# A gated attention and routed-expert kernel on one core: weight chunks split during the first stage, base products before the gather, quantisation maxima in PSUM

## The chip, the cores and the metric

The program runs on one core of one Trainium2 chip. The core has five engines with a queue each: TensorE (PE, matrix products and transposes into PSUM), VectorE (DVE), ScalarE (ACT), GpSimd (POOL) and SyncE (SP, which here only issues DMAs). Work in different queues is ordered by semaphores alone; inside one queue it runs in the order in which it was written. The metric is device time in microseconds (us) of one launch; less is better.

## The reference, cut to what matters

Two residual blocks follow each other on 4 x 256 tokens of width 256. The first is an int8 "smooth quant" two-layer product (four batches), the second routes every token to 2 of 8 experts.

```python
def _smooth_quant_linear(x, w):
    amax_x, amax_w = jnp.max(jnp.abs(x), axis=0), jnp.max(jnp.abs(w), axis=0)
    s = jnp.maximum(jnp.sqrt(jnp.maximum(amax_x, EPS) / jnp.maximum(amax_w, EPS)), EPS)
    xs, ws = x / s, w * s
    x_scale = jnp.maximum(jnp.max(jnp.abs(xs), axis=-1, keepdims=True), EPS) / QMAX
    w_scale = ...                      # the same over ws
    return round(xs / x_scale) @ round(ws / w_scale).T * x_scale * w_scale.T

x = x + tanh(g_xattn) * smooth_quant_expert(layernorm(x), fside, ctx)      # first stage
x2 = layernorm(x)
conf = sigmoid(x2 @ conf_W.T + conf_b); sel, routing = top-2 of conf * wealth
base_g, base_u = x2 @ base_gate, x2 @ base_up                              # 256 -> 896, all tokens
for e in range(8):
    g = base_g + x2 @ gate_A[e] @ gate_B[e] / 4
    u = base_u + x2 @ up_A[e] @ up_B[e] / 4
    h = silu(g) * u
    out += weight_e * (h @ base_down + h @ down_A[e] @ down_B[e] / 4)
x = x + tanh(g_ffn) * out
```

## The kernel before

There are two stages and a routing plan between them.

**First stage.** Each of the four batches b runs the same chain: layer norm, transposes on TensorE, maxima over the transposed banks on VectorE (`weights_amax`, `rows_amax`, `gated_amax`, `context_amax`), square roots on GpSimd (`roots1`, `roots2`), scaling on ScalarE, products, dequantisation, residual, a second layer norm (`stats2`, then `deviations2` on GpSimd, then `normal2` on ScalarE). The four batches are interleaved by hand: every engine's queue is written out call by call. Maxima go to small SBUF tiles (`amx`, `am1`, `am2`), from which a chain of small VectorE instructions (`ratio`: maximum with EPS, reciprocal, product, maximum; L894 to L899) makes the factors.

**Weights of the second stage.** They are needed as pairs of rounded numbers (`_hi`, `_lo`). SyncE loads them in 41 chunks of at most 128 x 512 through a ring `raw` of 4 slots. ScalarE copies a chunk to `_hi` (`split`, L579), GpSimd subtracts to get `_lo` (`split_lo`, L440), and only then is the slot loaded again (L391). Chunks 0 to 7 are base_gate and base_up, 8 to 11 the A matrices, 12 to 20 down_A and down_B, 21 to 28 gate_B, 29 to 36 up_B (`CH_1` is 37), the last four base_down. On GpSimd 12 chunks are placed among the calls of the first stage, then `lo(CH_1 - lo_done[0])` (L505) does the other 25. The first two gathers stand behind that line in the same queue.

**Base products.** `base_half(t, gu)` on TensorE makes one half (gate or up) of the 256 -> 896 product of token tile t (8 tiles): 12 products of 448 columns. ScalarE copies each half to `brow` and stores it to HBM. Tiles 0 to 5 (`PRE` is 6) stand ahead of the plan; tiles 6 and 7 stand behind the transposition `x_T(0)` of the first gathered tokens.

**The plan.** Logits of the four batches (`conf_rows`, then the transposes at L1472), sigmoid, top 2 on VectorE (L1038 to L1052, giving `pickb`), ranks on TensorE (L1483 to L1487, `s_rank`), places on VectorE (L1066 to L1080), two one-hot tables (`atrow` L1081, `attrib` L1083 to L1088), a sorting product on TensorE (L1496, `s_sorted`), and the indices `tok` and `dest` (L1106, `s_plan`).

**Second stage.** 19 tiles of 128 token-expert pairs: gather (`gather`, L511), project, expand, silu, product, transpose (`h_T`, L1548), down products, scatter. Tile 0 makes its base products directly from the gathered rows (L1606 to L1610, `s_direct`), because the stored rows are not ready then; `gather_base` fetches them for later tiles and waits for `s_direct`.

## Time and profile before

| | us |
|---|---|
| median of 3 runs | 347.58 (346.81 to 350.02) |
| the profiled execution's own time | 349.11 |
| its span, first to last instruction | 347.2 |
| TensorE busy | 261.5 (75%) |
| VectorE busy | 201.3 (58%) |
| ScalarE busy | 167.1 (48%) |
| GpSimd busy | 133.8 (39%) |

The busy shares are means over stages that have different limits. The page also prints the span in 40 slices of 8.7 us (each digit is the busy share in tenths; PEclk is the clock that TensorE was granted, in tenths of full speed):

```profile
PE   2569547988981003995999999999999999997700
POOL 5396614220057995018233333333333333311111
PEclk9855997899996555898999999999999999999755
```

TensorE has nothing to do in slices 12 to 15, which are the same slices in which GpSimd is full. Behind them the second stage holds TensorE at nine tenths until almost the end.

### The profile page before, as it was taken

How to read it: one execution, taken by the hardware profiler on the slowest of the kernel's cores; microseconds unless marked ns; L12 is line 12 of the kernel's file. 1: busy time of each engine (PE TensorE's matmuls, PEld its weight loads, DVE VectorE, ACT ScalarE, POOL GpSimd, SP SyncE). 2: the span in 40 equal slices, each digit the busy share in tenths (PEclk: the TensorE clock that was granted, in tenths of full speed). 3: DMA queues.
4: the chain of work that ended last, by engine and by line, in shares of the span. 5: the costliest groups of instructions: out<-in, count | busy, mean ns of one | idle time of the engine just before them, and what ended most of it. 6: DMA issues, size and time to landing. Idle time of an engine off the chain costs nothing.

```text
span 347.2 us, 5197 instructions
## 1 busy us (share of the span) xinstructions
PE 261.5 (75%) x1540; PEld 236.1 (68%) x1541; DVE 201.3 (58%) x409; ACT 167.1 (48%) x285; POOL 133.8 (39%) x162
## 2 busy tenths in 40 slices
PE   2569547988981003995999999999999999997700
PEld 1446435877971002994999999999999999996600
DVE  4598997661497000016667767777777677776115
ACT  2448875756354351253555545555555555555011
POOL 5396614220057995018233333333333333311111
PEclk9855997899996555898999999999999999999755
DMA  8545210025348674226244444444444444400065
GB/s 255 166 124 124 62 31 30 32 106 206 161 154 248 189 206 127 105 120 217 83 135 146 139 130 137 142 138 139 143 141 135 144 137 138 145 21 15 17 205 173
DMA packets 30190, 45.69 MB, mean 132 GB/s; under 512 B 13976, under 2 KB 25632, under 8 KB 30176
## 3 DMA queue, kind: packets, MB, share of 16 engines
q0 software_dynamic: 4416, 21.50, 18.7%
q1 hardware_dynamic: 21840, 14.55, 14.8%
q10 hardware_dynamic: 3920, 9.46, 7.2%
q8 instruction: 8, 0.13, 0.2%
q14 instruction: 6, 0.05, 0.0%
HBM read 33.57 MB, written 11.93 MB: 131 GB/s over the span
## 4 chain that ended last, share of the span: by engine, by line
PE 62%; DVE 10%; DMA 10%; POOL 6%; ACT 6%; issue 3%; SPq 2%; ACTq 0%; DVEq 0%
PE pY L55 8%; PE pY L59 7%; PE pY L57 7%; PE pG L55 5%; PE pT L1548 4%; PE pG L57 4%; PE pG L59 4%; PE pU L57 3%; PE pU L59 3%; PE pU L55 3%; DMA q<-in_ctx_dram 3%; PE bank L1254 2%; DMA yr<-results 2%; DMA raw<-in_L_ffn_down_A_dram 2%; POOL WdA_lo L440 2%
## 5 line engine op out<-in xcount | busy, mean ns | idle before, releaser
L525 POOL DMA_INDIRECT results<-yb,dest x19 | 18.8, 987 | 94.4 <-DVE yb L1188 94.4
L55 PE MATMUL pY<-Wd_hi,hT_hi 128*128 128x384 f32 x133 | 48.3, 363 | 1.1 <-ACT Wd_lo L789 0.8
L59 PE MATMUL pY<-Wd_hi,hT_lo 128*128 128x384 f32 x133 | 45.3, 341 | 0.0
L57 PE MATMUL pY<-Wd_lo,hT_hi 128*128 128x384 f32 x133 | 45.3, 341 | 0.0
L519 POOL DMA_INDIRECT bin<-base_products,tok x18 | 22.0, 1220 | 26.9 <-PE pU L59 17.1
L799 ACT CAST hT_hi<-pT 128x896 fp32r<-128x896 f32 x19 | 17.2, 907 | 24.1 <-PE pT L1548 24.1
L1511 PE MATMUL pX<-ident,xin 128*128 128x128 f32 x38 | 7.5, 280 | 27.9 <-DMA xin<-normed,tok 27.9
L55 PEld LDWEIGHTS pY<-Wd_hi,hT_hi 128*128 128x128 f32 x133 | 25.4, 191 | 3.3 <-issue 1.0
L775 ACT CAST xaT_hi<-pX 128x256 fp32r<-128x256 f32 x19 | 7.1, 374 | 42.5 <-PE pX L1525 42.1
L1118 DVE TENSOR_TENSOR xT_lo<-pX,xT_hi 128x256 fp32r<-128x256 f32 x19 | 7.9, 416 | 31.0 <-ACT xT_hi L769 31.0
L57 PEld LDWEIGHTS pY<-Wd_lo,hT_hi 128*128 128x128 f32 x133 | 25.6, 193 | 0.0
L59 PEld LDWEIGHTS pY<-Wd_hi,hT_lo 128*128 128x128 f32 x133 | 25.5, 191 | 0.0
L1511 PEld LDWEIGHTS pX<-ident,xin 128*128 128x128 f32 x38 | 5.3, 143 | 29.5 <-issue 28.0
L1261 PE MATMUL bank<-ident,q 128*128 128x128 f32 x80 | 16.9, 361 | 11.1 <-DMA q<-in_fside_BxS2xS_dram 6.4
L1172 DVE TENSOR_TENSOR hbuf<-hbuf,gb 128x896 f32<-128x896 f32 x19 | 22.6, 1192 | 1.9
L511 POOL DMA_INDIRECT xin<-normed,tok x19 | 18.6, 981 | 11.6 <-PE pX L1511 6.7
L1176 DVE TENSOR_TENSOR hT_lo<-pT,hT_hi 128x896 fp32r<-128x896 f32 x19 | 20.5, 1082 | 2.8 <-ACT hT_hi L799 2.8
L1261 PEld LDWEIGHTS bank<-ident,q 128*128 128x128 f32 x80 | 12.5, 185 | 14.2 <-issue 4.3
L1548 PE MATMUL pT<-ident,hbuf 128*128 128x128 f32 x133 | 18.4, 280 | 4.2 <-DVE hbuf L1172 4.2
L1145 DVE TENSOR_TENSOR xaT_lo<-pX,xaT_hi 128x256 fp32r<-128x256 f32 x19 | 8.1, 424 | 23.1 <-ACT xaT_hi L775 23.1
L793 ACT ACTIVATE gb<-gb 128x896 f32<-128x896 f32 x19 | 18.1, 954 | 6.6 <-DVE gb L1159 6.4
L1182 DVE TENSOR_TENSOR zT_lo<-pX,zT_hi 128x128 fp32r<-128x128 f32 x19 | 5.5, 292 | 25.9 <-ACT zT_hi L806 25.9
(234 smaller groups left out, 778.4 us busy)
## 6 DMA issues: line engine op xcount, KB each, us to landing
base_products<-brow ACTq DMA_DIRECT2D x8, 896.0 KB, 3.6
yr<-results SPq DMA_DIRECT2D x8, 256.0 KB, 5.4
raw<-in_L_ffn_down_A_dram SPq DMA_DIRECT2D x7, 256.0 KB, 3.0
raw<-in_L_ffn_gate_B_dram SPq DMA_DIRECT2D x8, 224.0 KB, 2.8
...
```

Of the source, the lines that this page charges most:

```text
L55: m.matmul(outs[i], hi, whi[i], start=first, stop=False, skip_group_check=True)
L57: m.matmul(outs[i], hi, wlo[i], start=False, stop=False, skip_group_check=True)
L59: ins = m.matmul(outs[i], lo, whi[i], start=False, stop=last, skip_group_check=True)
L511: g.indirect_dma_start(out=xin[:, :], out_offset=None, in_=xn, in_offset=bass.IndirectOffsetOnAxis(ap=tok[:, j:j + 1], axis=0)).then_inc(d ...
L519: g.indirect_dma_start(out=bin_[:, j % 2].rearrange("p a i -> p (a i)"), out_offset=None, in_=gun, in_offset=bass.IndirectOffsetOnAxis(ap= ...
L525: g.indirect_dma_start(out=yg, out_offset=bass.IndirectOffsetOnAxis(ap=dest[:, j:j + 1], axis=0), in_=yb[:, :], in_offset=None).then_inc(d ...
L793: a.activation(gb[:, :], gb[:, :], ACT.Silu).then_inc(s_silu, 1)
L799: a.copy(hT_hi[:, :, :].rearrange("p c q -> p (c q)"), pT[:, :, :].rearrange("p a q -> p (a q)")[:, 0:I]).then_inc(s_hhi, 1)
L1172: v.tensor_tensor(hbuf[:, :], hbuf[:, :], gb[:, :], ALU.mult).then_inc(s_h, 1)
L1176: v.tensor_tensor(hT_lo[:, :, :].rearrange("p c q -> p (c q)"), pT[:, :, :].rearrange("p a q -> p (a q)")[:, 0:I], hT_hi[:, :, :].rearrang ...
L1261: ins = m.transpose(bank[:, c * S + j * P:c * S + (j + 1) * P], rows_[:, j, c * P:(c + 1) * P], ident[:, :])
L1548: ins = m.transpose(pT[:, c // 4, (c % 4) * P:(c % 4 + 1) * P], hbuf[:, c * P:(c + 1) * P], ident[:, :])
```

## The change

It does four things. Splits are placed among the calls of the first stage and of the plan on ScalarE and GpSimd, and the ring has 6 slots. Base products of tiles 6 and 7 stand ahead of the plan's last wait, the rank products come one half earlier, and tile 0's direct products are split in two around `xa_T(0)`. Maxima are left in PSUM and the quotient chains have fewer instructions (reciprocals of the weights' and context's maxima are made ahead in `rcp_w` and `rcp_c`; the epsilon of the layer norm is added by a reduction). Nothing is left out of the computation.

```diff
-        RING, RW = 4, 512
+        RING, RW = 6, 512
@@ gpsimd, behind roots1(3) and lo(1)
             roots2(1)
+            lo(4)
             gated(2)
             deviations2(0)
+            lo(1)
             roots2(2)
+            lo(1)
             gated(3)
             deviations2(1)
+            lo(1)
             roots2(3)
+            lo(4)
             deviations2(2)
+            lo(1)
             deviations2(3)
             lo(CH_1 - lo_done[0])
@@ scalar
             integers_w(2)
-            split(1)
+            split(3)
             scaled2(0)
             scales_w(2)
             integers2(0)
+            split(1)
             scales_c(0)
+            split(1)
...
             normal2(0)
+            split(1)
             scales_w(3)
             x2_hi(0)
+            split(1)
             silu1(3)
+            split(2)
...
             integers2(2)
+            split(1)
...
             integers2(3)
+            split(1)
             base_half(1, 0)
             scales_c(3)
+            split(1)
             normal2(2)
             base_half(1, 1)
             base_store(1)
+            split(1)
             x2_hi(2)
             normal2(3)
...
             conf_rows(3)
+            split(1)
             act.wait_ge(s_logit, 1)
             a.activation(bids[:, :, :], bids[:, :, :], ACT.Sigmoid).then_inc(s_sig, 1)
+            split(2)
             base_half(3, 0)
+            split(1)
             base_half(3, 1)
             base_store(3)
+            split(2)
             base_half(4, 0)
...
             base_half(5, 1)
             base_store(5)
-            split(2)
             split(CH_1)
+            for t in range(PRE, NT):
+                base_out(t)
...
             x_hi(0)
-            for t in range(PRE, NT):
-                base_out(t)
             xa_hi(0, first=True)
@@ vector
             def weights_amax(b):
                 dve.wait_ge(s_wT, b + 1)
-                v.tensor_reduce(amx[:, b, 1, :], ...).then_inc(s_wamax, 1)
+                v.tensor_reduce(amx_w[:, b, :, 0], ...).then_inc(s_wamax, 1)
+                dve.wait_ge(s_wamax, b + 1)
+                link(v.tensor_reduce(rcp_w[:, b, :], amx_w[:, b, :, :], AX_X, ALU.max))
+                link(v.reciprocal(rcp_w[:, b, :], rcp_w[:, b, :]))
             def context_amax(b):
                 dve.wait_ge(s_cT, b + 1)
-                v.tensor_reduce(amx2[:, b, 1:2], beta(b)[:, 0:S], ...).then_inc(s_camax, 1)
+                c = beta(b)[:, S + 8:S + 9]
+                link(v.tensor_reduce(c, beta(b)[:, 0:S], AX_X, ALU.max, apply_absolute_value=True))
+                link(v.tensor_scalar(c, c, EPS, None, ALU.max))
+                v.reciprocal(rcp_c[:, b:b + 1], c).then_inc(s_camax, 1)
@@ statistics
-                v.tensor_scalar(vs, vs, LN_EPS, None, ALU.add).then_inc(made, 1)
+                v.tensor_reduce(wide[:, TB * b:TB * (b + 1)], mine[:, :, 1:3], AX_X, ALU.add).then_inc(made, 1)
@@ rows_amax; gated_amax likewise
-                ratio(amx[:, b, 0, :], amx[:, b, 1, :], amx[:, b], tmp8[:, b, :], s_ratio)
+                link(v.scalar_tensor_tensor(out=x_, in0=x_, scalar=EPS, in1=rcp_w[:, b, :], op0=ALU.max, op1=ALU.mult))
+                v.tensor_scalar(tmp8[:, b, :], x_, EPS * EPS, None, ALU.max).then_inc(s_ratio, 1)
@@ smooth1; smooth2 likewise
-                link(v.tensor_reduce(am1[:, b, :], q1[:, :, b, :], AX_X, ALU.max, apply_absolute_value=True))
-                scales(am1[:, b, :], inv1[:, b, :], sc1[:, b, :], s_inv1)
+                am = beta(b)[:, 0:4]
+                link(v.tensor_reduce(am, q1[:, :, b, :], AX_X, ALU.max, apply_absolute_value=True))
+                scales(am, inv1[:, b, :], sc1[:, b, :], s_inv1)
@@ tensor
             base_half(3, 1)
-            base_half(4, 0)
             pe.wait_ge(s_pickb, 1)
...
             ins.then_inc(s_rank, 1)
-            base_half(4, 1)
-            base_half(5, 0)
-            base_half(5, 1)
+            base(4)
+            base(5)
+            base_half(6, 0)
...
             ins.then_inc(s_sorted, 1)
+            base_half(6, 1)
+            base(7)
             pe.wait_ge(s_plan, 1)
...
             x_T(0)
-            base(PRE)
             pe.wait_ge(s_wlo, CH_A)
             project_A(0, group(0))
-            base(PRE + 1)
+            direct(0)
             xa_T(0)
-            for gu, copied in enumerate((s_bgc, s_buc)):
-                ...
-            ins.then_inc(s_direct, 1)
+            direct(1).then_inc(s_direct, 1)
```

What the change does to the queues stands at three places. The first is GpSimd's queue from the last square root of the first stage to the first gather (`_lo` rows are weight chunks, `rstd` and `nmr` the layer norm). Before:

```order
L476 TENSOR_TENSOR s_rs<-tmp,half 128x2
L453 TENSOR_TENSOR rstd<-mv,half 128x2
L456 TENSOR_SCALAR nmr<-mv,rstd 128x1 x2
L453 TENSOR_TENSOR rstd<-mv,half 128x2
L456 TENSOR_SCALAR nmr<-mv,rstd 128x1 x2
L440 TENSOR_TENSOR WdA_lo<-raw,WdA_hi 128x512 x7
L440 TENSOR_TENSOR WdB_lo<-raw,WdB_hi 128x512 x2
L440 TENSOR_TENSOR WBg_lo<-raw,WBg_hi 128x448 x8
L440 TENSOR_TENSOR WBu_lo<-raw,WBu_hi 128x448 x8
L511 DMA xin<-normed,tok 128x256 x2
```

With the change:

```order
L481 TENSOR_TENSOR s_rs<-tmp,half 128x2
L445 TENSOR_TENSOR WdB_lo<-raw,WdB_hi 128x512 x2
L445 TENSOR_TENSOR WBg_lo<-raw,WBg_hi 128x448 x2
L458 TENSOR_TENSOR rstd<-spread,half 128x2
L461 TENSOR_SCALAR nmr<-mv,rstd 128x1 x2
L445 TENSOR_TENSOR WBg_lo<-raw,WBg_hi 128x448
L458 TENSOR_TENSOR rstd<-spread,half 128x2
L461 TENSOR_SCALAR nmr<-mv,rstd 128x1 x2
L445 TENSOR_TENSOR WBg_lo<-raw,WBg_hi 128x448 x5
L445 TENSOR_TENSOR WBu_lo<-raw,WBu_hi 128x448 x8
L522 DMA xin<-normed,tok 128x256 x2
```

Of the 25 chunks that stood in one piece ahead of the gather 12 are now among the first stage's calls and 13 are left; five of the 12 stand ahead of the last two layer norms.

The second place is TensorE's queue at the rank products (`bank<-pickb` is their first row; `pG` and `pU` rows are base halves). Before:

```order
L59 MATMUL pU<-Wbase_hi,x2T_lo 128x448 x2
L55 MATMUL pG<-Wbase_hi,x2T_hi 128x448 x2
L57 MATMUL pG<-Wbase_lo,x2T_hi 128x448 x2
L59 MATMUL pG<-Wbase_hi,x2T_lo 128x448 x2
L55 MATMUL pG<-Wbase_hi,x2T_hi 128x448 x2
L57 MATMUL pG<-Wbase_lo,x2T_hi 128x448 x2
L59 MATMUL pG<-Wbase_hi,x2T_lo 128x448 x2
L1483 MATMUL bank<-pickb,beforeb 128x64
```

With the change:

```order
L57 MATMUL pU<-Wbase_lo,x2T_hi 128x448 x2
L59 MATMUL pU<-Wbase_hi,x2T_lo 128x448 x2
L1511 MATMUL bank<-pickb,beforeb 128x64
L1513 MATMUL bank<-pickb,onesb 128x60
L1513 MATMUL bank<-pickb,onesb 128x56
```

The half of tile 4 that stood between the end of tile 3 and the ranks now stands behind them.

The third place is TensorE's queue at the first gathered tile (`pX<-ident,xin`). Before:

```order
L1496 MATMUL bank<-attrib,atrow 128x76 x16
L1511 MATMUL pX<-ident,xin 128x128 x2
L55 MATMUL pG<-Wbase_hi,x2T_hi 128x448 x2
L57 MATMUL pG<-Wbase_lo,x2T_hi 128x448 x2
L59 MATMUL pG<-Wbase_hi,x2T_lo 128x448 x2
```

With the change:

```order
L59 MATMUL pU<-Wbase_hi,x2T_lo 128x448 x2
L1541 MATMUL pX<-ident,xin 128x128 x2
L1536 TENSOR_LOAD gid
L1536 ISA x2
L55 ISA
L55 MATMUL pX<-WA_hi,xT_hi 128x256
```

The four base halves of tiles 6 and 7 have gone from behind the gathered tile to ahead of it (three of them behind the sorting product, one before it), so that the projection follows the transposes at once.

## Rows read from the trace of the kernel before

**Rows 1.** Stages table: stage, its us; busy (x count) by engine, clock, DMA.

```profile
core 0: us, PE busy (x) PEld busy (x) DVE busy (x) ACT busy (x) POOL busy (x), PEclk, DMA share, GB/s
56.00:87.00 31.00, 27.02 (x157) 22.38 (x155) 16.90 (x51) 19.65 (x39) 6.55 (x12) 0.94 0.28 108
...
97.00:110.50 13.50, 6.63 (x43) 5.71 (x41) 13.02 (x24) 6.66 (x10) 8.49 (x6) 0.87 0.77 246
110.50:132.80 22.30, 0.00 (x0) 0.00 (x0) 0.10 (x1) 10.23 (x19) 21.31 (x19) 0.50 0.64 177
...
162.30:317.30 155.00, 154.68 (x961) 145.88 (x962) 107.52 (x175) 79.56 (x123) 53.86 (x51) 0.99 0.38 124
```

**Rows 2.** GpSimd in order of time: start, us, what, [idle before <-releaser].

```profile
18.01 1.02 POOL L467 TENSOR_TENSOR s_rs<-tmp,half 128x4 f32<-128x4 f32 x1
...
74.19 0.70 POOL L453 TENSOR_TENSOR rstd<-mv,half 128x2 f32<-128x2 f32 x1 [9.56 <-DVE mv L884]
...
77.15 0.71 POOL L453 TENSOR_TENSOR rstd<-mv,half 128x2 f32<-128x2 f32 x1 [1.23 <-DVE mv L884]
...
99.66 8.49 POOL L440 TENSOR_TENSOR WdA_lo<-raw,WdA_hi 128x512 fp32r<-128x512 f32 x6 [21.20 <-ACT WdA_hi L579]
...
132.83 1.21 POOL L511 DMA_INDIRECT xin<-normed,tok  x1 [0.19 <-issue]
```

**Rows 3.** VectorE in the plan, in order of time.

```profile
86.70 0.22 DVE L1034 TENSOR_TENSOR bids<-bank,rows 128x64 f32<-128x64 f32 x1 [3.19 <-PE bank L1472]
...
90.73 0.20 DVE L1052 CAST pickb<-gp 128x64 bf16<-128x64 f32 x1
...
95.12 0.16 DVE L1066 TENSOR_SCALAR tiles_g<-bank 128x4 f32<-128x4 f32 x1 [3.76 <-PE bank L1487]
...
97.71 2.29 DVE L1081 TENSOR_TENSOR atrow<-prow,fcol 128x2048 bf16<-128x2048 f32 x1
99.92 1.57 DVE L1083 TENSOR_TENSOR attile<-ptile,fcol 128x304 f32<-128x304 f32 x1
...
110.28 0.18 DVE L1106 TENSOR_SCALAR tok<-dest 128x19 int32<-128x19 int32 x1
```

**Rows 4.** TensorE in order of time.

```profile
89.15 0.57 PE L55 MATMUL pU<-Wbase_hi,x2T_hi 128*128 128x448 f32 x2
...
91.60 0.57 PE L55 MATMUL pG<-Wbase_hi,x2T_hi 128*128 128x448 f32 x2
...
94.05 0.20 PE L1483 MATMUL bank<-pickb,beforeb 128*128 128x64 bf16 x1
...
107.17 1.17 PE L1496 MATMUL bank<-attrib,atrow 128*128 128x76 bf16 x16 [4.72 <-DVE attrib L1088]
136.22 0.66 PE L1511 MATMUL pX<-ident,xin 128*128 128x128 f32 x2 [27.88 <-DMA xin<-normed,tok]
136.54 1.09 PE L55 MATMUL pG<-Wbase_hi,x2T_hi 128*128 128x448 f32 x2
...
141.16 0.58 PE L55 MATMUL pU<-Wbase_hi,x2T_hi 128*128 128x448 f32 x2
...
154.30 0.38 PE L1511 MATMUL pX<-ident,xin 128*128 128x128 f32 x2
...
162.27 1.76 PE L1548 MATMUL pT<-ident,hbuf 128*128 128x128 f32 x7 [4.18 <-DVE hbuf L1172]
```

**Rows 5.** ScalarE in order of time.

```profile
75.96 1.09 ACT L588 ACTIVATE q<-x_resid,nmr,rstd 128x256 f32<-128x256 f32 x2 [1.86 <-POOL nmr L456]
...
97.60 0.91 ACT L661 COPY brow<-pU 128x896 f32<-128x896 f32 x1 [2.24 <-PE pU L59]
...
98.96 1.14 ACT L579 CAST WdA_hi<-raw 128x512 fp32r<-128x512 f32 x2 [0.45 <-ACT brow L661]
```

**Rows 6.** VectorE in the first stage: the same small instruction twice.

```profile
14.91 0.83 DVE L896 TENSOR_SCALAR amx<-amx 128x4 f32<-128x4 f32 x1
...
20.79 0.18 DVE L896 TENSOR_SCALAR amx<-amx 128x4 f32<-128x4 f32 x1
```

More of the change, by code:

```diff
@@ L139, in build @@
             bst = s1("bst", [P, NT, 6])
-            mv = s1("mv", [P, NT, 2])
+            mv = s1("mv", [P, NT, 3])
+            spread = s1("spread", [P, NT])
             rstd = s1("rstd", [P, NT])
@@ L143, in build @@
             half = s1("half", [P, 2, HC])
-            amx = s1("amx", [P, NB, 2, HC])
+            amx_w = s1("amx_w", [P, NB, HC, 2])
+            rcp_w = s1("rcp_w", [P, NB, HC])
             s_rs = s1("s_rs", [P, NB, 2, HC])
             tmp8 = s1("tmp8", [P, NB, HC])
-            am1 = s1("am1", [P, NB, 4])
             inv1 = s1("inv1", [P, NB, 4])
             sc1 = s1("sc1", [P, NB, 4])
-            amx2 = s1("amx2", [P, NB, 2])
+            rcp_c = s1("rcp_c", [P, NB])
             s_rs2 = s1("s_rs2", [P, NB, 2])
             tmp4 = s1("tmp4", [P, NB])
-            am2 = s1("am2", [P, NB, 4])
+            step = s1("step", [P, 1])
             inv2 = s1("inv2", [P, NB, 4])
@@ L157, in build @@
             bst2 = s1("bst2", [P, NT, 6])
-            mv2 = s1("mv2", [P, NT, 2])
+            mv2 = s1("mv2", [P, NT, 3])
+            spread2 = s1("spread2", [P, NT])
             rstd2 = s1("rstd2", [P, NT])
@@ L424, in _ @@
                 g.memset(rounder[:, i:i + 1], value).then_inc(s_rounder, 1)
+            g.memset(amx_w[:, :, :, 1], EPS).then_inc(s_eps, 1)
+            for moments in (mv, mv2):
+                g.memset(moments[:, :, 2], LN_EPS).then_inc(s_eps, 1)
             for i, value in enumerate((-0.5, 0.5)):
@@ L447, in lo, with deviations @@
                     lo_done[0] += 1
-            def deviations(b, source, made, root, rooted, product, done_):
+            def deviations(b, source, wide, made, root, rooted, product, done_):
                 ts = slice(TB * b, TB * (b + 1))
                 pool.wait_ge(made, b + 1)
-                g.tensor_tensor(root[:, ts], source[:, ts, 1], half[:, 0, 0:TB], ALU.pow).then_inc(rooted, 1)
+                g.tensor_tensor(root[:, ts], wide[:, ts], half[:, 0, 0:TB], ALU.pow).then_inc(rooted, 1)
                 pool.wait_ge(rooted, b + 1)
@@ L747, in _ @@
             a.activation(share[:, 1, :], dif[:, :], ACT.Sigmoid, scale=-1.0).then_inc(s_share, 1)
+            split(2)
             base_half(4, 1)
@@ L934, in gated_amax @@
                 dve.wait_ge(s_camax, b + 1)
-                v.tensor_reduce(amx2[:, b, 0:1], alpha(b)[:, 0:S], AX_X, ALU.max, apply_absolute_value=True).then_inc(s_aamax, 1)
+                a_ = alpha(b)[:, S:S + 1]
+                v.tensor_reduce(a_, alpha(b)[:, 0:S], AX_X, ALU.max, apply_absolute_value=True).then_inc(s_aamax, 1)
                 dve.wait_ge(s_aamax, b + 1)
-                ratio(amx2[:, b, 0:1], amx2[:, b, 1:2], amx2[:, b], tmp4[:, b:b + 1], s_ratio2)
+                link(v.tensor_scalar(a_, a_, EPS, rcp_c[:, b:b + 1], ALU.max, ALU.mult))
+                v.tensor_scalar(tmp4[:, b:b + 1], a_, EPS * EPS, None, ALU.max).then_inc(s_ratio2, 1)
             def smooth2(b):
@@ L945, in smooth2 @@
                 dve.wait_ge(s_smooth2, b + 1)
-                link(v.tensor_reduce(am2[:, b, :], q2[:, b], AX_X, ALU.max, apply_absolute_value=True))
-                scales(am2[:, b, :], inv2[:, b, :], sc2[:, b, :], s_inv2)
+                am = beta(b)[:, 0:4]
+                link(v.tensor_reduce(am, q2[:, b], AX_X, ALU.max, apply_absolute_value=True))
+                scales(am, inv2[:, b, :], sc2[:, b, :], s_inv2)
                 if b == 0:
                     dve.wait_ge(s_gate, 1)
-                v.tensor_scalar(sc2g[:, b, :], sc2[:, b, 0:2], gates[:, 0:1], None, ALU.mult).then_inc(s_sc2g, 1)
+                    link(v.tensor_scalar(step[:, :], gates[:, 0:1], 1.0 / QMAX, None, ALU.mult))
+                v.tensor_scalar(sc2g[:, b, :], am[:, 0:TB], EPS, step[:, :], ALU.max, ALU.mult).then_inc(s_sc2g, 1)
             def dequantise2(b):
@@ L975, in logit_weights @@
                 v.tensor_tensor(cWT_lo[:, :, :], pc, cWT_hi[:, :, :], ALU.subtract).then_inc(s_cWT, 1)
+            dve.wait_ge(s_eps, 3)
             stats1(0)
@@ L1597, in tile, with direct @@
                 h_T(j)
+            def direct(gu):
+                pe.wait_ge((s_bgc, s_buc)[gu], NT)
+                for c in range(HC):
+                    ins = base_product((pG, pU)[gu], gu, c, xT_hi[:, c, :], xT_lo[:, c, :], False)
+                return ins
             x_T(0)
-            base(PRE)
             pe.wait_ge(s_wlo, CH_A)
             project_A(0, group(0))
-            base(PRE + 1)
+            direct(0)
             xa_T(0)
-            for gu, copied in enumerate((s_bgc, s_buc)):
-                pe.wait_ge(copied, NT)
-                for c in range(HC):
-                    ins = base_product((pG, pU)[gu], gu, c, xT_hi[:, c, :], xT_lo[:, c, :], False)
-            ins.then_inc(s_direct, 1)
+            direct(1).then_inc(s_direct, 1)
             pe.wait_ge(s_xalo, 1)
```

28 lines of the change are left out of this document (11 added, 17 removed).

## The prediction

> **What bounds the kernel now.** I read the table by stages first, because the busy shares of the page are means. TensorE is busy for 154.68 of the 155 us of the tile loop, but for nothing at all from 110.5 to 132.8 us, where GpSimd is busy for 21.31 of 22.3 us [rows 1]. Then GpSimd in order of time: what fills that stretch are the `_lo` subtractions of weight chunks, begun at 99.66 us, and the first gather follows the last of them with 0.19 us between [rows 2]. The plan that the gather needs was ready at 110.46 us (`tok`, 110.28 + 0.18) [rows 3]. So the gather was 22.4 us late, held by the order of GpSimd's queue and by nothing else. Then TensorE: it waits 27.88 us for the gathered rows, transposes them at 136.22, computes the base halves of tiles 6 and 7, and finishes tile 0's direct products at 154.30 [rows 4]. The reader is to see two separate costs: weights ahead of the gather, and work that needs no gather placed behind it.
>
> **The sum** is made in times of the profiled execution (span 347.2, its own time 349.11) and then carried to the median of the runs (347.58, which is 1.53 lower). I call C the moment at which VectorE starts on the logits, 86.70 now [rows 3]. A base half costs TensorE 91.60 - 89.15 = 2.45 us at the full clock; the first one after the long idle takes 141.16 - 136.54 = 4.6 us [rows 4].
>
> *First stage, shift of C.* VectorE gains. Eight quotient chains lose two small instructions of 0.18 us and a gap each, about 0.4 per chain or 3.2 together; `context_amax` gets two more in four places, 1.6; those of `weights_amax` lie in waits for loads. And the same small instruction took 0.83 us at 14.91, while GpSimd subtracted, and 0.18 at 20.79 [rows 6]: kept in PSUM I take it to be free of that wait, 0.65 us each at about five places, 3.3. That is 4.9 at most. But GpSimd's own order binds the first two batches (`roots1(0)` at 18.01 starts without any wait, straight behind three subtractions [rows 2]), so I take 3.0 (bounds 0 and 4.9). ScalarE loses: 13 more splits before C at 1.14 / 2 = 0.57 us [rows 5] are 7.4 us. Between 56 and 87 us it has 31 - 19.65 = 11.35 us idle [rows 1], mostly waiting for others, so I cost the splits at 1.0 in the crowded part around 48 us and nothing behind; without that cover it would be all 7.4. GpSimd loses at the end: `lo(4)` ahead of `deviations2(2)` waits for a split that ScalarE does behind `scales_c(3)`, at about 74.1; split 0.57 and subtraction 1.13 end at 75.9 instead of the present start at 74.19 [rows 2]. `lo(1)` ahead of `deviations2(3)` waits for ScalarE's `normal2(2)` (1.09, starting 1.7 later than its 75.96), a brow copy (0.91), a store (0.4) and a split (0.57) [rows 5], plus the subtraction: 81.8 instead of 77.15. Queued behind it are the last `normal2`, the last `x2_T` and all logits; 3.8 us of the 4.6 reach them. Sum: -3.0 + 1.0 + 3.8 = +1.8, C = 88.5 (bounds: -4.9 and +11.2).
>
> *Top 2 and ranks.* Now `pickb` is ready at 90.93, C + 4.2, and the ranks wait for one more half, until 94.05 = C + 7.35 [rows 3, 4]. Moved one half earlier they could start at C + 4.9. But now six subtractions (13 are left at C, two splits after nearly every half) fall into the same VectorE chain. What one such neighbour costs stands in the plan's second half: five instructions of 304 elements, from 99.92 until the sorting product's release at 107.1, take 7.2 / 5 = 1.43 us each while GpSimd runs six subtractions in 8.49 us, and one of 2048 elements, begun before them, took only 2.29 [rows 2 to 4]. By size the five would be 0.35 each, so a subtraction costs the chain 1.1. The Trainium skill has a rule for it (SBUF — State Buffer, "Who interferes with whom"): a VectorE instruction with two SBUF inputs blocks against a GpSimd instruction that reads SBUF, for the whole instruction, and a PSUM operand avoids it. By that rule the maxima in PSUM are right and the subtractions placed into the top 2 are wrong; the trace agrees with 1.43 us against 0.35. I let 4 to 5 of the six cost their 1.13: `pickb` at C + 9.4, with TensorE idle from C + 4.9 (bounds: C + 4.2, none costs; C + 11.0, all do).
>
> *After that idle.* The engine comes back slowly: after 4.18 us of idle seven transposes took 1.76 us, and after 27.88 us the first half cost 4.6 instead of 2.45, a loss of 2.15 [rows 4]. I take 1.7 (bounds 0 and 2.15).
>
> *To the first transpose.* Ranks 0.8 to 0.9, five halves 12.25, sorting product 1.17 [rows 4], three halves 7.35. C + 9.4 + 0.9 + 1.7 + 12.25 + 1.2 + 7.35 = C + 32.8 = 121.3. What lies beside it: VectorE's tables, 2.6 + 2.3 + 7.2 behind the ranks, end at C + 22.4, 1.9 before the five halves do. GpSimd's last subtraction stands behind the split after half (5,1), about C + 24.8; the plan, 1.7 behind the sorting product, is ready at C + 27.2; the gather lands 136.22 - 132.83 = 3.4 later [rows 2, 4], at C + 30.7, 2.1 us before TensorE is free. So the gather is hidden, and TensorE's queue sets the time. The transpose moves from 136.22 to 121.3, 14.9 us.
>
> *Behind it.* 154.30 - 136.22 = 18.1 us now. It loses the four halves, 4.6 + 3 x 2.45 = 12.0. It gains what they covered: the copy and store of tile 7's last half, which stand ahead of `xT_hi` on ScalarE (0.91 + 0.4 [rows 5]), and two short casts with their gaps, of which 2.2 are exposed (bounds 0.9 and 3). 8.3 us, a gain of 9.8.
>
> *The rest* keeps its length: nothing in it changes, TensorE fills it [rows 1], and tile 0's silu, product and splits of base_down are released by `s_direct` as before (8 us, to 162.27 [rows 4]).
>
> 14.9 + 9.8 = 24.7. Span 322.5; own time 324.4; against the median 347.58 - 24.7 = **322.9 us**.
>
> **Rivals.**
> 1. *The collisions cost nothing* (20%). For it: a subtraction starts only when its split is done, so GpSimd is not always busy there. Ranks at C + 4.9, no slow clock, transpose at C + 26.6. With C + 1.8 that is 115.1, gain 21.1 + 9.8 = 30.9: 316.7 us; with C at 83.7 as well (its gain of 3.0 and neither loss) 311.9.
> 2. *The first stage pays more* (15%). ScalarE and GpSimd queues are in order, and the splits are not hidden: 7.4 instead of 1.0, C = 94.9. Gain 18.3: 329.3 us. Against it: ScalarE's 11.35 us idle.
> 3. *Weights are still last* (7%). 13 chunks remain at C, each waiting for a load, a split and 1.13 us. Were GpSimd done only 6 us behind the plan (C + 33 instead of 24.8), the gather would land at C + 36.6 and the gain shrink by 3.8 to 20.9 (326.7), and more if loads are late. The cover is 2.4 us against the plan and 2.1 behind it.
> 4. *Slower than before* (1.5%). Twelve subtractions now stand ahead of roots and layer norms in GpSimd's order; if the loads for them came late each would hold the first stage. It decides when they cost more than 24.7 / 12 = 2.1 us each; at 3 us each the time is 322.9 + 36 = 358.9 us. Against it: the ring is loaded long ahead there, GpSimd idles 9.56 us before 74.19 [rows 2].
> 5. *No effect* (1.5%): the gather would have to wait for something that stays at 132 us; the plan at 110.46 excludes it.
>
> **How the numbers follow.** The forecast has 55% and its own range is 319 to 327. Rival 1 reaches to 312, rival 2 to 331 and beyond; 316 to 331 leaves about a fifth out. A measurement here tells 1% from no change: faster by over 1% is everything below 344, 0.97; within 1% 0.015; slower 0.015.
>
> **What would show it.** C at 88.5 (step one); `pickb` 9.4 behind C with TensorE idle before L1511 (step two), against 4.2 if rival 1 holds; VectorE instructions of 1.3 us in the top 2; `x_T(0)` released by TensorE's own queue and not by the gather; 8.3 us from it to `x_T(1)`; 193 us behind that. A gather behind the last subtraction without a gap, later than the plan, would make rival 3 true.

## The result, and the profile after

| | median us (lowest to highest), executions | ratio to before, 95% |
|---|---|---|
| before | 347.20 (346.81 to 350.02), 4 | |
| with the change | 321.02 (320.74 to 321.65), 4 | 0.9232 [0.9181, 0.9284] |
| the same again, beside other kernels | 321.16 (319.75 to 322.52), 6 | 0.9250 [0.9219, 0.9281] |

The forecast was 322.9 us. The profiled execution of before took 349.11 us and that of after 320.75, spans 347.2 and 318.9; that the gain is 28.3 us in the spans and 26.2 in the medians is for the greater part the profiled execution of before, which lay 1.9 above its median.

The page of after, its span, its busy shares and the slices of TensorE and its clock:

```profile
span 318.9 us, 5202 instructions
PE 261.7 (82%) x1540; PEld 236.2 (74%) x1541; DVE 200.2 (63%) x410; ACT 164.8 (52%) x285; POOL 134.3 (42%) x165
...
PE   2568558897879979499999999999999999997500
...
PEclk9999996798998999879999999999999999998955
```

A slice is 8 us, counted here from one (the empty slices of before are then its 13th to 16th). The stretch in which TensorE did nothing is gone: from the 12th slice (88 us) to the 36th no digit is under 7, but for one 4 (128 to 136 us, the pause before the first `h_T`, which before has too). Behind C the clock row dips at the 13th slice and at the 17th and 18th, behind two of the pauses that are left. The table by stages, with the stretches of after that answer to [rows 1]:

```profile
core 0: us, PE busy (x) PEld busy (x) DVE busy (x) ACT busy (x) POOL busy (x), PEclk, DMA share, GB/s
56.00:87.70 31.70, 27.06 (x147) 22.62 (x148) 14.95 (x42) 21.61 (x42) 15.23 (x20) 0.89 0.47 155
94.40:109.00 14.60, 14.59 (x98) 13.42 (x99) 13.40 (x25) 8.00 (x16) 10.09 (x9) 0.88 0.67 226
109.00:125.30 16.30, 14.11 (x85) 12.63 (x82) 3.75 (x16) 5.84 (x8) 2.98 (x3) 1.00 0.53 203
133.20:144.20 11.00, 10.92 (x51) 10.26 (x52) 5.08 (x8) 4.18 (x6) 3.78 (x4) 0.72 0.11 37
```

From the ranks to the transpose of the second gathered tile (94.4 to 125.3 us) TensorE is now busy for 28.7 of 30.9 us; the 22.3 us in which it was empty lay in this part. Up to C, GpSimd does 15.23 us instead of 6.55 of [rows 1] in nearly the same length: that is the weight work which has moved.

TensorE in order of time, the answer to [rows 4]:

```profile
94.41 0.20 PE L1511 MATMUL bank<-pickb,beforeb 128*128 128x64 bf16 x1 [1.76 <-DVE pickb L1081]
...
95.25 1.09 PE L55 MATMUL pG<-Wbase_hi,x2T_hi 128*128 128x448 f32 x2
...
99.17 0.56 PE L55 MATMUL pU<-Wbase_hi,x2T_hi 128*128 128x448 f32 x2
...
108.78 0.73 PE L1524 MATMUL bank<-attrib,atrow 128*128 128x76 bf16 x16
...
117.37 0.41 PE L1541 MATMUL pX<-ident,xin 128*128 128x128 f32 x2 [0.56 <-DMA xin<-normed,tok]
119.41 0.38 PE L55 MATMUL pX<-WA_hi,xT_hi 128*128 x1 [1.63 <-DVE xT_lo L1147]
...
125.32 0.38 PE L1541 MATMUL pX<-ident,xin 128*128 128x128 f32 x2
...
133.28 1.76 PE L1578 MATMUL pT<-ident,hbuf 128*128 128x128 f32 x7 [4.17 <-DVE hbuf L1201]
```

VectorE in the plan, the answer to [rows 3]:

```profile
87.67 0.22 DVE L1063 TENSOR_TENSOR bids<-bank,rows 128x64 f32<-128x64 f32 x1 [3.17 <-PE bank L1501]
...
88.99 0.96 DVE L1070 TENSOR_TENSOR eq<-bids,best 128x64 f32<-128x64 f32 x1
89.99 1.08 DVE L1071 TENSOR_TENSOR eq<-eq,tiebreak 128x64 f32<-128x64 f32 x1
...
92.13 0.82 DVE L1070 TENSOR_TENSOR eq<-bids,best 128x64 f32<-128x64 f32 x1
92.99 0.23 DVE L1071 TENSOR_TENSOR eq<-eq,tiebreak 128x64 f32<-128x64 f32 x1
...
94.16 0.20 DVE L1081 CAST pickb<-gp 128x64 bf16<-128x64 f32 x1
...
106.44 1.27 DVE L1117 CAST attrib<-attile 128x304 bf16<-128x304 f32 x1
...
111.44 0.18 DVE L1135 TENSOR_SCALAR tok<-dest 128x19 int32<-128x19 int32 x1
```

GpSimd beside it, the answer to [rows 2]:

```profile
78.41 1.15 POOL L445 TENSOR_TENSOR WBg_lo<-raw,WBg_hi 128x448 fp32r<-128x448 f32 x1 [3.03 <-ACT WBg_hi L590]
...
87.47 3.52 POOL L445 TENSOR_TENSOR WBg_lo<-raw,WBg_hi 128x448 fp32r<-128x448 f32 x3 [6.65 <-ACT WBg_hi L590]
91.73 1.15 POOL L445 TENSOR_TENSOR WBg_lo<-raw,WBg_hi 128x448 fp32r<-128x448 f32 x1 [0.74 <-ACT WBg_hi L590]
...
101.02 8.81 POOL L445 TENSOR_TENSOR WBu_lo<-raw,WBu_hi 128x448 fp32r<-128x448 f32 x7 [4.08 <-ACT WBu_hi L590]
112.67 1.21 POOL L522 DMA_INDIRECT xin<-normed,tok  x1 [2.84 <-DVE share L1137]
```

The reader is to see three things. The gather at 112.67 no longer follows a subtraction; it waits, 2.84 us, for the plan. The last four subtractions ahead of `pickb` (87.47 to 92.88) stand beside the VectorE instructions of 0.82 to 1.08 us, while their twin at 92.99, with GpSimd idle, took 0.23. And TensorE, which had no pause before the ranks [rows 4], now has one of 1.76 us, behind which a base half took 99.17 - 95.25 = 3.92 us instead of 2.40. This last thing is not the same in each execution. TensorE at the same place in the repeat:

```profile
94.79 0.65 PE L55 MATMUL pG<-Wbase_hi,x2T_hi 128*128 128x448 f32 x2
...
97.28 0.56 PE L55 MATMUL pU<-Wbase_hi,x2T_hi 128*128 128x448 f32 x2
```

The pause was 1.77 us there and the half took 97.28 - 94.79 = 2.49 us, at a granted clock of 1.00 (93.95 to 98.80 us) instead of 0.64.

### The profile page after: what moved, and what is told of

Read it like the earlier page. It is cut to its first block, busy times and chain, and to the rows that moved or that the text cites. A ratio compares the mean times of both kernels' runs of the same rounds, so it can differ in the third digit from the quotient of the medians.

```text
span 318.9 us, 5202 instructions
## 1 busy us (share of the span) xinstructions
PE 261.7 (82%) x1540; PEld 236.2 (74%) x1541; DVE 200.2 (63%) x410; ACT 164.8 (52%) x285; POOL 134.3 (42%) x165
## 4 chain that ended last, share of the span: by engine, by line
PE 68%; ACT 10%; DMA 5%; DVE 5%; POOL 5%; issue 3%; SPq 2%; ACTq 0%; DVEq 0%
PE pY L55 9%; PE pY L57 8%; PE pY L59 8%; PE pG L55 5%; PE pT L1578 5%; PE pG L57 5%; PE pG L59 5%; PE pU L55 4%; PE pU L57 4%; PE pU L59 4%; DMA raw<-in_L_ffn_base_gate_dram 3%; PE bank L1283 2%; DMA yr<-results 2%; PE pX L55 1%; POOL Wbase_lo L445 1%
## 5 line engine op out<-in xcount | busy, mean ns | idle before, releaser
L818 ACT ACTIVATE gb<-gb 128x896 f32<-128x896 f32 x19 | 18.1, 954 | 5.6 <-DVE gb L1188 5.4
L1578 PEld LDWEIGHTS pT<-ident,hbuf 128*128 128x128 f32 x133 | 16.2, 145 | 5.0 <-DVE hbuf L1201 4.4
L1188 DVE TENSOR_TENSOR gb<-pG,bin 128x896 f32<-128x896 f32 x18 | 19.5, 1081 | 0.2 <-PE pG L59 0.2
L1196 DVE TENSOR_TENSOR hbuf<-pU,bin 128x896 f32<-128x896 f32 x18 | 19.4, 1080 | 0.0
```

The costliest lines, as they stand in the source:

```text
L1188: v.tensor_tensor(halves(gb[:, :]), pG[:, :, 0:IH], halves(bin_[:, slot, 0, :]), ALU.add).then_inc(s_gadd, 1)
L1196: v.tensor_tensor(halves(hbuf[:, :]), pU[:, :, 0:IH], halves(bin_[:, slot, 1, :]), ALU.add).then_inc(s_uadd, 1)
L1578: ins = m.transpose(pT[:, c // 4, (c % 4) * P:(c % 4 + 1) * P], hbuf[:, c * P:(c + 1) * P], ident[:, :])
```

## The experiments

The kernels p, those with q and those with r ran as three groups, each on one chip and beside runs of before (medians 346.98, 347.30 and 346.80). "The whole" is the kernel with the change. Its repeat ran beside the q kernels (321.16); the p and r kernels are set against it across groups. `x_T(0)` and `x_T(1)` are TensorE's transposes of the first two gathered tiles.

| kernel | median us (range) | ratio to before, 95% | C | `x_T(0)` | `x_T(1)` |
|---|---|---|---|---|---|
| before | 347.20 (346.81 to 350.02) | | 86.70 | 136.22 | 154.30 |
| the whole | 321.02 (320.74 to 321.65) | 0.9232 [0.9181, 0.9284] | 87.67 | 117.37 | 125.32 |
| its repeat | 321.16 (319.75 to 322.52) | 0.9250 [0.9219, 0.9281] | 87.22 | 116.25 | 125.39 |
| p1_splits | 334.11 (332.89 to 335.22) | 0.9619 [0.9564, 0.9674] | 92.77 | 121.88 | 139.97 |
| p2_base | 342.91 (342.62 to 343.62) | 0.9884 [0.9835, 0.9932] | 85.10 | 138.86 | 148.89 |
| p3_psum | 342.32 (341.02 to 344.23) | 0.9850 [0.9794, 0.9907] | 82.26 | 131.83 | 149.33 |
| p4_splits_base | 323.23 (322.50 to 325.80) | 0.9332 [0.9270, 0.9394] | 92.26 | 121.41 | 129.22 |
| q1_ring4 | 321.89 (319.66 to 322.88) | 0.9253 [0.9216, 0.9289] | 88.72 | 119.25 | 126.75 |
| q2_rank_later | 324.44 (322.04 to 325.32) | 0.9321 [0.9283, 0.9358] | 88.43 | 120.83 | 129.51 |
| q3_plan_psum | 317.33 (316.69 to 319.11) | 0.9143 [0.9109, 0.9177] | 87.50 | 114.65 | 122.29 |
| r1_plan_all | 319.48 (319.15 to 320.28) | 0.9208 [0.9175, 0.9241] | 88.94 | 115.98 | 124.66 |
| r2_lo_behind | 316.75 (315.84 to 316.89) | 0.9119 [0.9087, 0.9151] | 84.05 | 113.02 | 122.27 |
| r3_wd_early | 316.71 (314.97 to 318.26) | 0.9114 [0.9060, 0.9167] | 88.18 | 117.90 | 125.85 |
| r4_best | 313.77 (311.30 to 315.49) | 0.9018 [0.8971, 0.9065] | 85.70 | 112.75 | 122.99 |

C and the two transposes are each from one profiled execution. Traces with the same code up to C differ: before has 86.70 and p2_base 85.10; the seven of the change's family whose calls up to C are in the same order (after and its repeat, q1, which has only a smaller ring there, q2, q3, r1, r3) have 87.2 to 88.9, mean 88.1. So a difference of C under 1.7 us between two traces says nothing; intervals counted from C say more.

### The three parts of the change, apart and together

The first four kernels start from before. **p1_splits** has only the ring of six and the splits and subtractions in the first stage (ScalarE's rows correspond):

```diff
+            lo(4)
             gated(2)
             deviations2(0)
+            lo(1)
...
             roots2(3)
+            lo(4)
             deviations2(2)
+            lo(1)
             deviations2(3)
```

> The kernel before with the split placement and the ring of 6 alone (base products, maxima and quotient chains as before). Theory (the weights in front of the gather cost 14.9 of the 24.7 us that were forecast, the moved base products 9.8): the gather is released by the plan; without the PSUM maxima the first stage has only its losses, C (VectorE's first logits instruction, 86.70 before, 87.67 with the whole change) at about 90.5; the transpose of the first gathered tile at C + 28 = 118.5, and 18.1 us behind it as before: 347.4 - 17.5 = 330 us, range 327 to 334. Rival (all of the gain hangs on the gather, the base products were covered anyway): 321 to 323 us.

It gained 12.9 us (346.98 to 334.11) and ended 4 us above the expected 330, just outside its range. C is at 92.77, 6.1 us behind before's and 2.3 behind the expected 90.5, and the plan then ran into GpSimd's subtractions. VectorE in p1_splits, the small chain behind the ranks:

```profile
101.17 0.16 DVE L1084 TENSOR_SCALAR tiles_g<-bank 128x4 f32<-128x4 f32 x1 [1.24 <-PE bank L1505]
...
107.99 3.18 DVE L1099 TENSOR_TENSOR atrow<-prow,fcol 128x2048 bf16<-128x2048 f32 x1
```

From `tiles_g` to `atrow` it took 6.8 us instead of 97.71 - 95.12 = 2.6 [rows 3], and TensorE waited 6.34 us before the sorting product, since it has no more base halves there. What follows `x_T(0)` is 18.1 us long as before.

**p2_base** has only the order of the base products: those of tiles 6 and 7 ahead of the gather, the ranks one half earlier, the direct products in two halves, and the copies of the moved halves among the splits on ScalarE. At `x_T(0)`:

```diff
             x_T(0)
-            base(PRE)
             pe.wait_ge(s_wlo, CH_A)
             project_A(0, group(0))
-            base(PRE + 1)
+            direct(0)
             xa_T(0)
...
```

> The kernel before with the order of the base products alone (tiles 6 and 7 ahead of the first gathered tile, their copies placed among the splits on ScalarE, ranks one half earlier). Theory: the gather stays at 132.8 us and the transpose at 136.2; behind it 18.1 us become 8 plus what the slower clock after the idle costs here, 2 to 3 us, since direct products now fall into it: gain 7 to 8.5 us, 339 to 340.5 us. Rival (moved work was covered): 346 to 348 us. If the copies among the splits delay the last subtraction, the gather comes that much later; more than 1 us of it would show in the trace.

A miss: it gained 4.1 us, not 7 to 8.5. Behind `x_T(0)` it gained 8.1 (10.0 us instead of 18.1, at a granted clock of 0.66 after a wait of 17 us). But the weights are later. TensorE at `x_T(0)` and GpSimd at the first gather, in p2_base:

```profile
138.86 0.66 PE L1519 MATMUL pX<-ident,xin 128*128 128x128 f32 x2 [17.02 <-DMA xin<-normed,tok]
```

```profile
135.71 1.21 POOL L511 DMA_INDIRECT xin<-normed,tok  x1 [0.18 <-issue]
```

The gather is at 135.71 against 132.83 [rows 2], 4.5 us later counted from C, held by the same queue. So half of what the order of TensorE gives is paid back as long as the weights are last. The copies of four base halves now stand among the splits on ScalarE (0.90 us each), but the last three splits ahead of the gather also wait 3.39 us for a load; how much of the delay is the copies' own is not shown.

**p3_psum** has only the maxima in PSUM and the shorter chains (`amx`, `am1`, `am2` go, as in the change).

> The kernel before with the maxima in PSUM and the shorter quotient chains alone. Theory: C falls by about 3 us (bounds 0 and 4.9), and all that follows moves with it, since the splits of the second part start behind C: 344 to 345 us. Rival (GpSimd's and ScalarE's own order binds the first stage, VectorE has slack): C within 0.7 us, 347 us.

It gained 4.7 us, where 2 to 3 were expected. VectorE's first instruction on the logits in p3_psum:

```profile
82.26 0.22 DVE L1045 TENSOR_TENSOR bids<-bank,rows 128x64 f32<-128x64 f32 x1 [3.17 <-PE bank L1483]
```

C is 4.4 earlier than in before's trace and 2.8 earlier than in p2_base's; the gather came 4.1 earlier (128.69), and the median moved by 4.7. The gains of p2 and p3 are under 2%, but their intervals lie clear of 1.

**p4_splits_base** is the whole without the maxima in PSUM, so p1 and p2 together, with the copies of tiles 6 and 7 placed behind the splits as in the change.

> The whole change without the maxima in PSUM (split placement, ring of 6, base order). Theory: 3 us of C are lost against the whole change (321.0 us), 324 us, and small VectorE instructions next to subtractions take up to 1.1 us again. Rival (VectorE has slack): 321 to 322 us.

It gained 23.8 us (323.23 for an expected 324). The parts alone give 12.9 + 4.1 + 4.7 = 21.7, the whole 26: p1 and p2 together are worth 23.8 where they are 17.0 apart. The base halves fill the wait of 6.34 us that p1 has before the sorting product (0.20 in p4), and with p1's splits the gather no longer waits for weights. From p4 to the whole C falls from 92.26 to a mean of 88.1, but the median by 2.1 to 2.2 only. Where the rest goes differs between the whole's two traces: against p4, after's loses 0.7 us between C and the first `h_T` and 1.7 behind it (183.9 us in p4, 185.6 in after), its repeat's 1.2 and 0.7. No run says why.

### Where the collision with GpSimd costs, and what takes it away

The next three start from the whole. **q1_ring4** puts the ring back to four buffers.

```diff
-        RING, RW = 6, 512
+        RING, RW = 4, 512
```

> The whole change with 4 ring slots instead of 6. Theory (loads are issued long ahead of their splits in the first stage, a load takes 2.5 to 3 us there): at most 1 us, 321 to 322 us. Rival (each split waits for a load that a subtraction released only just before): C later by 2 us or more, 323 to 326 us.

321.89 against 321.16 with intervals that overlap: the two more buffers have no effect that these runs can tell. **q2_rank_later** puts one half of tile 4 back ahead of the ranks, where TensorE was idle:

```diff
             base_half(3, 1)
+            base_half(4, 0)
 
             pe.wait_ge(s_pickb, 1)
...
-            base(4)
+            base_half(4, 1)
             base(5)
```

> The whole change, but with one half of tile 4 ahead of the rank products again, as before. Theory (pickb is late by 2.5 us because of the subtractions, so ranks placed earlier only make TensorE idle and slow): the half fills the 1.8 us idle, the next half does not run at the lower clock; now VectorE's tables set the sorting product, at C + 20.3 instead of C + 21.1: 320.2 us. Rival (the earlier ranks are worth their half, 2.4 us): 323 us.

A miss: 324.44, 3.3 us slower than the whole instead of 1 faster. The pause before the ranks is gone, as expected, yet the time got longer. VectorE, TensorE and GpSimd in q2_rank_later:

```profile
96.72 0.16 DVE L1095 TENSOR_SCALAR tiles_g<-bank 128x4 f32<-128x4 f32 x1 [1.16 <-PE bank L1516]
...
104.61 3.20 DVE L1110 TENSOR_TENSOR atrow<-prow,fcol 128x2048 bf16<-128x2048 f32 x1
```

```profile
110.68 1.17 PE L1525 MATMUL bank<-attrib,atrow 128*128 128x76 bf16 x16 [4.36 <-DVE attrib L1117]
```

```profile
96.55 3.39 POOL L445 TENSOR_TENSOR WBu_lo<-raw,WBu_hi 128x448 fp32r<-128x448 f32 x3
```

In the whole GpSimd is idle from 96.94 to 101.02 (4.08 us, for a split on ScalarE), just while VectorE goes from `tiles_g` to `atrow` in 98.99 - 95.50 = 3.5 us. With the half moved, ScalarE has its copy and then the splits earlier, and GpSimd's subtractions fall into that chain: 7.9 us. The sorting product waits 4.36 us, and the next base half runs at a low clock. One place of a table was moved and the collision went from the harmless place to the harmful one.

**q3_plan_psum** goes at the operands: the tables `bids`, `eq` and `attile` are kept in PSUM banks that are free there, so that the instructions have a PSUM operand; nothing is reordered.

```diff
+            bids_p = A[5][:, 0:NT * E].rearrange("p (t e) -> p t e", t=NT)
+            eq_p = A[5][:, NT * E:2 * NT * E].rearrange("p (t e) -> p t e", t=NT)
+            attile_p = A[4][:, 0:NG * PT].rearrange("p (g j) -> p g j", g=NG)
...
-                link(v.tensor_tensor(eq[:, :, :], eq[:, :, :], tiebreak_b, ALU.mult))
+                link(v.tensor_tensor(eq_p, eq_p, tiebreak_b, ALU.mult))
```

> The whole change, with the top 2 tables (bids, eq) and the tile table (attile) of the plan in idle PSUM banks, so that each VectorE instruction on them has at most one SBUF input; instructions and subtractions are otherwise the same. Theory (the late pickb comes from VectorE waiting for GpSimd where it reads two SBUF inputs): the instructions on bids and eq take 0.25 instead of up to 1.08 us, those on attile 0.4 instead of 1.3 to 1.4, pickb at C + 4.5, ranks at C + 4.9 with no idle and no slow half, sorting product 3.2 us earlier, 317.8 us. Rival (VectorE is slowed by something else, such as its own clock or the semaphores): durations and time unchanged, 321 us.

317.33, as expected. VectorE, GpSimd and TensorE in q3_plan_psum:

```profile
88.54 0.23 DVE L1073 TENSOR_TENSOR bank<-bank,best 128x64 f32<-128x64 f32 x1
88.80 0.23 DVE L1074 TENSOR_TENSOR bank<-bank,tiebreak 128x64 f32<-128x64 f32 x1
...
91.77 0.98 DVE L1084 CAST pickb<-gp 128x64 bf16<-128x64 f32 x1
...
103.78 0.48 DVE L1117 TENSOR_TENSOR attrib<-bank,fcol 128x304 bf16<-128x304 f32 x1
```

```profile
87.30 3.49 POOL L445 TENSOR_TENSOR WBg_lo<-raw,WBg_hi 128x448 fp32r<-128x448 f32 x3 [6.65 <-ACT WBg_hi L590]
```

```profile
92.81 0.20 PE L1514 MATMUL bank<-pickb,beforeb 128*128 128x64 bf16 x1 [0.33 <-DVE pickb L1084]
```

The same comparison that took 0.96 us takes 0.23, the product behind it 0.23 instead of 1.08, and a table of 304 elements 0.48 instead of 1.32, with the same subtractions beside them. What was left in SBUF still collides (`pickb` 0.98; `atrow` 3.19 instead of 2.29, and from `tiles_g` to `atrow` 5.3 us instead of 3.5). TensorE's pause is 0.33 instead of 1.76 us, and `x_T(0)` comes at C + 27.2 instead of C + 29.7 (C + 29.0 in the repeat). The clock behind the pause is 1.00, but that it is in the repeat without this edit too. This bears out the rule of the Trainium skill (SBUF — State Buffer, "Who interferes with whom") that the prediction weighed, both its loss and its remedy.

**r1_plan_all** goes further: the rest of the small chain in PSUM (but for `csum`, `start_g` and `placef`), and the sorting product two halves earlier.

```diff
-            floor_of(tiles_g[:, :], A[7][:, CNT:CNT + G], 1.0 - 1.0 / P)
+            floor_of(tiles_p, A[7][:, CNT:CNT + G], 1.0 - 1.0 / P)
...
             base(4)
-            base(5)
-            base_half(6, 0)
+            base_half(5, 0)
```

> The run with the plan's tables in PSUM, with four more small ones there (tiles, places, tile and row numbers) and the sorting product behind three halves instead of five. Theory: with VectorE free of the subtractions its tables end at C + 14, so the sorting product can stand earlier, the gather lands before the last base half is done (about C + 22 against C + 26), and the transpose of the first gathered tile follows TensorE's own queue at C + 26 instead of C + 27.2: 316.0 us against 317.3. Rival (the sorting product has to wait for tables at this place, an idle of 3 us or more and slow halves behind it): 320 us.

A miss: 319.48 for an expected 316.0, no better than q3's 317.33, and not by the rival's wait of 3 us either. TensorE and GpSimd in r1_plan_all:

```profile
103.34 0.72 PE L1530 MATMUL bank<-attrib,atrow 128*128 128x76 bf16 x16 [0.81 <-DVE attrib L1124]
...
115.98 0.38 PE L1548 MATMUL pX<-ident,xin 128*128 128x128 f32 x2
118.74 0.38 PE L55 MATMUL pX<-WA_hi,xT_hi 128*128 x1 [2.38 <-DVE xT_lo L1154]
```

```profile
108.58 1.16 POOL L445 TENSOR_TENSOR WBu_lo<-raw,WBu_hi 128x448 fp32r<-128x448 f32 x1 [1.96 <-ACT WBu_hi L590]
109.92 1.21 POOL L522 DMA_INDIRECT xin<-normed,tok  x1 [0.18 <-issue]
```

The sorting product came at C + 14.4 instead of q3's C + 18.2, and `x_T(0)` at C + 27.0 instead of C + 27.2: it has no wait any more, the ranks, eight halves and the sorting product fill TensorE's queue up to it. So the plan had ceased to be the bound with q3, and the 0.9 us of wait that was left turned into a longer one behind: the projection now waits 2.38 us instead of 1.30, because the copy and the store of tile 7 still stand ahead of `xT_hi` on ScalarE. Here, too, the gather follows the last subtraction (the prediction's rival 3), and it costs nothing. Of the 2.4 us by which r1's trace is longer than q3's, 1.4 lie ahead of C, where the code is the same but for names, and 1.0 between `x_T(0)` and `x_T(1)` (8.68 instead of 7.64). Why C is later is open.

### Two edits that follow from the trace of after

**r2_lo_behind** puts two subtractions one place later each: one goes from ahead of `deviations2(2)` to ahead of `deviations2(3)`, and the one whose split was late (the wait of 3.03 us before 78.41 above) from there to behind both:

```diff
             roots2(3)
-            lo(4)
+            lo(3)
             deviations2(2)
```

> The whole change, with two of the five subtractions that stand ahead of the last two layer norms of GpSimd put one place later each (chunk 22 between them, chunk 23 behind both); nothing else. Theory (of the first stage's losses 3.8 us come from these two): stats of batch 3 are ready at 75.5 and its deviations follow at once instead of 4.0 us later, C at about 84 instead of 87.7, 317.5 to 318 us. Rival (ScalarE's queue, not GpSimd's, carries the loss): C within 1 us, 320.5 to 321 us.

316.75, 4.3 us under the whole and 0.8 better than expected. GpSimd in r2_lo_behind:

```profile
74.56 0.71 POOL L458 TENSOR_TENSOR rstd<-spread,half 128x2 f32<-128x2 f32 x1
```

The second layer norm's `rstd` is at 74.56 instead of 79.52. Of the 4.96 us, 4.0 reach C, counted from the family's mean of 88.1 (3.6 from after's own). Two subtractions one place too early in GpSimd's queue cost about what the maxima in PSUM had brought. The two were not moved apart; that it is mostly the second follows from the waits in after, 0.78 us for the split ahead of the first `rstd` and 3.03 for that ahead of the second.

**r3_wd_early** moves the last four splits of base_down and their subtractions ahead of the first tile's silu, out of the way of `h_mul`:

```diff
             x_hi(0)
-            xa_hi(0, first=True)
...
             for i in range(2):
                 act.wait_ge(d_bn[i], 16 * NT // 2)
             split(NCH - CH_1, NCH)
+            xa_hi(0, first=True)
...
```

> The whole change, with the splits of base_down (4 chunks) ahead of xa_hi(0) on ScalarE and ahead of the first gather_base on GpSimd, so that they are over before tile 0's product of silu and up. Theory (that product, 2.97 us against a mean of 1.19, and the transposes at the low clock behind a 4.2 us idle are the same collision as in the plan): product 1.1 us, idle 2.3 us, 318 to 319 us. Rival (the gathers of base products that are now 1 us later come too late for tile 1): 321 us or more.

316.71, 4.3 us under the whole, more than expected. VectorE and TensorE in r3_wd_early:

```profile
130.80 1.08 DVE L1201 TENSOR_TENSOR hbuf<-hbuf,gb 128x896 f32<-128x896 f32 x1
```

```profile
131.94 0.98 PE L1578 MATMUL pT<-ident,hbuf 128*128 128x128 f32 x7 [2.29 <-DVE hbuf L1201]
```

The product of 896 elements, both inputs in SBUF, took 2.95 us in after, beside four subtractions, and 1.08 here. TensorE's pause falls from 4.17 to 2.29, and the seven transposes behind it from 1.76 to 0.98: from `x_T(1)` to `h_T(0)` 6.1 instead of 8.0 us, from there to the next `h_T` 9.8 instead of 10.4 to 10.8 in after, its repeat and q1 to q3. From `x_T(0)` to the end it is 198.1 instead of 201.5, 3.4 of the 4.3. The pause of 4.18 us stands in before as well [rows 4]; the prediction had it inside its "8 us" and asked no further.

**r4_best** is q3, r1, r2 and r3 together.

> The three together. If each acts on its own place: 321.1 - 3.8 - 1.3 - 3.3 - 2.5 = 310.2 us, range 308.5 to 313. If they share one limit, no better than the best of them, 316.

313.77 [ratio 0.9018, 0.8971 to 0.9065], 7.3 us under the whole and the best of all, but 3.6 over its expectation and outside its range. C is at 85.70, not at r2's 84, and from `x_T(0)` to `x_T(1)` it took 10.24 us, where after has 7.95. The table by stages of r4_best, from the projection behind `x_T(0)` to `x_T(1)` (the columns are those of the table above):

```profile
115.50:123.00 7.50, 7.50 (x33) 6.82 (x34) 0.85 (x2) 3.83 (x7) 4.09 (x4) 0.77 0.26 96
```

A wait of 2.38 us for `xT_lo` as in r1 (0.75 more than after's 1.63), and then a granted clock of 0.77 (1.5 us): 7.95 + 0.75 + 1.5 = 10.2. r2 had that low clock too, 0.78 after a wait of 1.41; r1 had none, 1.00 after the same 2.38. It does not even belong to the kernel: the whole had 1.00 there after 1.63, and its repeat, the same code, 0.78 after 1.35 (7.38 us for the work that took after 5.91). What decides it these runs don't show.

## Why the prediction was right, point by point

**Its result and its sign** hold: 322.9 against 321.0. The mechanism does too: the gather was held by the order of GpSimd's queue (p1, which changes only the places of the weight work and the ring, brings it from 132.83 to 118.76; q1 finds no effect of the ring), and the base halves behind `x_T(0)` were the second cost (8.1 us in p2). Against the spans the sum was 3.6 short (24.7 for 28.3), which is made of the following.

**C, the first stage.** Predicted 88.5; measured 87.67, and 88.1 as the mean of seven traces. But its terms were too small in part. The maxima in PSUM were put at 3.0 and give 2.8 to 4.4 alone, 3.3 to 5.0 beside the subtractions (p4 against the seven traces); the splits were put at 4.8 and cost 5.6 to 7.7 (p1 and p4 against the two traces with before's first stage). The errors are of opposite sign, and that they cancelled in C is luck. `lo(1)` ahead of `deviations2(3)` was right: a wait of 3.03 us for the split, and `rstd` behind it at 79.52, where 81.8 less the 3.0 of the maxima and with the 1.0 of the splits is 79.8. r2 shows that the price hangs on one place in GpSimd's queue.

**Top 2.** Predicted C + 9.4, measured C + 6.7: here the term was twice too large. The row says why: four subtractions touch the chain (87.47 to 92.88), and only where a two-input instruction begins in them. They cost 2.5 us together, 0.6 each and not 1.13: two of the four instructions end at 91.07 and 92.95, just behind the ends of subtractions at 90.99 and 92.88, so each pays what is left of a subtraction when it begins. The fifth and sixth start at 94.70, because their splits stand behind base-half copies on ScalarE. The step that failed is "I let 4 to 5 of the six cost their 1.13": the neighbours were counted by the queue and not by when their own releaser lets them start, and each was priced at its full length. Rival 1 had named that reason.

**The clock behind the pause** was put at 1.7 and cost 3.92 - 2.40 = 1.5 in after, but 2.49 - 2.40 = 0.1 in its repeat. Six traces have this pause, of 1.72 to 1.77 us: three show a granted clock of 0.64 behind it (after, q1, r3) and three 1.00 (the repeat, p4, r2). That the term fits the trace of after is luck. It moves `x_T(0)` by 0.7 us only, from C + 29.7 to the repeat's C + 29.0, because without it the sorting product waits for the tables (0.37 us).

**To `x_T(0)`.** Predicted C + 32.8 and released by TensorE's own queue, measured C + 29.7 and released by the gather with 0.56 us of wait. 2.7 of the 3.1 are the top 2. The tables ended at 107.71, C + 20.0, and hid as predicted; GpSimd's last subtraction ended at 109.83, C + 22.2, 1.8 before the plan (111.62): rival 3 was false. The gather was not hidden because it needs longer than I took, in two parts. 0.19 us is what it took behind work that ran; one that waits starts 112.67 - 111.62 = 1.05 us after `tok`, behind `share`, whose 0.23 us end at 111.76, so 0.9 us after its own release. And from its start to the transpose it took 117.37 - 112.67 = 4.70 us (4.02 in the repeat), not the 3.4 of before; why it is longer there no run shows. Rival 1's arithmetic, C + 26.6 without collisions, is nearly met by the kernels with fewer of them (r1 C + 27.0, q3 C + 27.2).

**Behind it.** Predicted 8.3, measured 7.95 in after and 9.14 in its repeat, which had the low clock here instead. The casts between `x_T(0)` and its projection show as the wait of 1.63 for `xT_lo` (1.35 in the repeat).

**The rest** was to keep its length: 193.6 in after and 192.5 in its repeat, against 192.9. The stretch from the first `h_T` to the next is 10.8 us instead of 9.3 [rows 4, for its start]; behind the pause of 4.17 more of its expand products take 0.57 us instead of 0.37 (granted clock 0.72 from 133.2 to 144.2). It is hardly an effect of the change: p3, whose order there is that of before, has 10.7 (157.30 to 168.04), p2 10.8, and of the twelve traces with this pause only before's and p1's have 9.3 to 9.4. That the clock comes back later in one execution than in another is seen; why is open.

**Span against median.** The sum was carried to the median by subtracting it from 347.58. The profiled execution of before lay 1.9 over the median of the result, and after's 0.3 under its own: the gain is 28.3 in the spans and 26.2 in the medians, which takes 2.1 of the 3.6 away again. The median of before is 347.20 in the result, 0.4 lower than in the forecast, and 1.9 are left. The forecast came nearer than its terms, by luck.
